# Skip term of a fused recurrent layer: a bf16 diagonal matmul and ScalarE seeds replaced by one fp32 VectorE pass per bank

## The chip, the cores and the metric

The kernel runs on the 8 cores of one Trainium2 chip. Each core works on two of the 16 sequences by itself; no core waits for another. The metric is the device time in microseconds (us) of the slowest core, median of three runs. The engines of a core are TensorE (PE, its weight loads PEld), VectorE (DVE), ScalarE (ACT), GpSimd (POOL) and SyncE (SP), which here only issues DMAs.

## What is computed

For x of shape (16, 2048, 2048), with all weights given:

```
xn = layernorm(x)
# recurrent layer on xn
xn1 = layernorm(xn) * gamma + beta
u   = xn1 @ W_in + b_in                  # (.., 8)
h_t = sigmoid(decay_logit) * h_(t-1) + u_t
x1  = xn + h @ W_out + b_out + xn1 * D_skip
xn2 = layernorm(x1) * gamma + beta
s   = x1 + relu(xn2 @ W_down + b_down) @ W_up + b_up
# quantized layer on the same xn
y   = relu(fake_quant(xn) @ fake_quant(kernel) + fake_quant(bias))
g   = silu(fake_quant(y))
out = x + s * g
```

`fake_quant` rounds to 8 bits with one scale per row (per column for the kernel).

## The kernel before

A core has 32 tiles of 128 rows of x; tile c is rows of sequence c % 2. The program writes five instruction queues by hand (`P` for PE, `V` for DVE, `S` for ACT, `G` for POOL, `Y` for SP): each `put` appends to one engine's queue and names marks that it waits for. Nothing is moved by a scheduler, so an engine runs its queue strictly in the written order, and the order of the calls in the loop `for i in range(1, NCH + 1)` is the schedule. Before the loop stands a prologue that quantizes and transposes the 2048 x 2048 kernel and works on tiles 0 to 2.

The steps of one tile c, with the names that the rest of the text uses:

- `load_x` fetches the tile (128 x 2048, fp32, 1 MB) into one of four buffers `x0` to `x3`.
- `v_stats` and `v_mean` (DVE) give mean and variance, `g_norm` (POOL, nine one-column operations, L451 to L461) the factors of both norms. `s_center` (ACT, L474) writes x minus mean into `xc`, one of two buffers.
- `g_z` (POOL, L465) writes the twice normalized row as bf16, `turn_z` transposes it by DMA into `zT`. `v_amax` (DVE, L481 to L485: a maximum over 2048 and four one-column operations), `s_quant_x` (ACT) and `g_ixb` (POOL, L494) give the integers of the quantized row, which a second DMA transposes into `ixT`.
- The quantized product: four banks q of 512 columns, each 16 matmuls 128x512 (`p_half`, `p_part`, L519) on top of the bias that `s_bias` (ACT, L501) writes into PSUM bank `py0` or `py1`; `v_evac` (DVE, L527) scales the bank into `t1` and keeps a running maximum. `v_ymax` and `s_gate` (ACT: Relu to 8 bits, L541, then Silu over all 2048 columns, L542) give the gate `g`.
- The recurrent part: `p_low` (16 matmuls, L570), `v_low` (L585, L588), a transpose `p_uT`, `v_scan` (DVE, L598: the same scan twice, once into fp32 `h`, once into bf16 `haug`), then the sum x1 in the four PSUM banks `px`: `s_seed` (ACT, L550 and L554) writes a starting value into each bank, `v_skip` (DVE, L562) multiplies banks 0 and 1 by `xc`, `p_skip` (PE, L578: 8 matmuls 128x128 of `zT` with a diagonal bf16 matrix) adds the skip term of banks 2 and 3, and `p_out` (PE, L605, L608) adds h @ W_out.
- The second norm: `s_square` (ACT, L615) sums the squares of `px`; `g_rstd2` (POOL, L624 to L628) makes the factor r2 of it; `v_hidden` (DVE, L632), a transpose `p_hfT` (PE, L637), `v_hfa` (DVE, L640) and `p_up` (PE, L646) add the last product to `px`.
- The end: `v_gated` (DVE, L653) multiplies `px` by the gate into `g`, bank by bank, `g_add` (POOL, L658) adds that to x, and `store` writes the tile.

There is one `px`, so tile c+1 can be seeded only when tile c has been gated. In a loop body i, the gate and the adds belong to tile i-1, the product to tile i, the quantization to tile i+1, the norms to tile i+2.

## Time and profile before

| | |
|---|---|
| median of 3 runs | 605.12 us (605.01 to 605.27) |
| the profiled execution | 605.74 us |
| span of its slowest core (7), first to last instruction | 604.2 us |
| spans of the other cores | 600.9 to 603.8 us |
| PE busy / share of the span | 553.4 us, 92% |
| DVE | 510.8 us, 85% |
| ACT | 518.8 us, 86% |
| POOL | 443.8 us, 73% |
| granted TensorE clock, mean of core 7 | 0.971; 1.00 from 100 to 580 us |

A row of a timeline is: start in us, duration in us, engine, line, operation, output <- input, shape, count; a bracket at the end tells how long the engine was idle before and what ended that. Instructions in a row of one kind are merged. The start of the next row minus the start of this one is what an instruction costs in its queue. The stages: the prologue until about 100 us, 30 tiles in a fixed rhythm until about 590 us, and the last tile's end.

### The profile page before, as it was taken

Reading aid. Unit: us, or ns where it says so; the run is one execution under the profiler, and the core shown is the slowest. Engines: PE = TensorE matmul, PEld = TensorE weight load, DVE = VectorE, ACT = ScalarE, POOL = GpSimd, SP = SyncE. Lnnn points to the kernel's source line nnn. Section 1 sums busy time; section 2 is a strip of 40 time slices with the busy share of each in tenths; the row PEclk is TensorE's granted clock in tenths of the full one; section 3 lists DMA queues with packets and bytes.
Section 4 is the critical chain, followed back from the end, with each engine's and each line's share of the span. In section 5 each row is a group of like instructions: output and inputs, shape, how many; then the busy total and the mean of one; then the engine's idle time right before and its main releaser. Section 6 shows DMA issues by size and latency. Waiting matters only on the chain.

```text
span 604.2 us, 10061 instructions; the slowest of 8 cores (600.9 to 604.2 us)
## 1 busy us (share of the span) xinstructions
PE 553.4 (92%) x3538; PEld 272.1 (45%) x3538; DVE 510.8 (85%) x1181; ACT 518.8 (86%) x497; POOL 443.8 (73%) x709
## 2 busy tenths in 40 slices
...
GB/s 240 335 347 312 220 132 68 190 201 205 209 196 198 200 190 178 195 205 209 182 183 194 199 194 200 209 197 206 195 178 202 182 201 209 191 191 183 132 71 140
DMA packets 141683, 118.89 MB, mean 197 GB/s; under 512 B 130368, under 2 KB 130368, under 8 KB 131520
## 3 DMA queue, kind: packets, MB, share of 16 engines
...
q8 instruction: 28, 0.46, 0.3%
q14 instruction: 23, 0.19, 0.1%
...
## 4 chain that ended last, share of the span: by engine, by line
PE 84%; ACT 6%; DVE 5%; DMA 2%; issue 1%; POOL 1%; SPq 0%; ACTq 0%; DVEq 0%; POOLq 0%
PE py L519 71%; PE pu L570 3%; PE px L646 3%; DMA x<-L_attn_x 2%; PE px L578 2%; DVE kst L333 1%; PE px L367 1%; PE px L608 1%; ACT xc L474 1%; DVE t L441 1%; PE pt L637 1%; ACT junk L350 1%; ACT zix L490 1%; ACT kq L389 1%; ACT k L350 1%
## 5 line engine op out<-in xcount | busy, mean ns | idle before, releaser
L519 PE MATMUL py<-kq,ixT 128*128 128x512 bf16 x2048 | 462.9, 380 | 3.6 <-ACT py L501 3.2
L519 PEld LDWEIGHTS py<-kq,ixT 128*128 128x128 bf16 x2048 | 194.3, 98 | 228.2 <-ACT py L501 12.9
L658 POOL TENSOR_TENSOR x<-x,g 128x512 f32<-128x512 f32 x124 | 155.1, 1272 | 56.6 <-DVE g L653 54.2
L615 ACT ACTIVATE junk<-px 128x2048 bf16<-128x2048 f32 x32 | 60.1, 1877 | 49.5 <-PE px L608 49.5
L527 DVE CUSTOM_DVE_ANT_0 t<-py,sc_bc,st 128x512 f32<-128x512 f32 x96 | 71.5, 745 | 21.7 <-PE py L519 21.6
L501 ACT ACTIVATE py<-brow,st 128x512 f32<-128x512 f32 x128 | 86.6, 677 | 3.8 <-DVE st L527 2.9
L441 DVE BATCH_NORM_STATS2 t<-x 128x6 f32<-128x512 f32 x128 | 81.5, 681 | 2.8 <-DMA x<-L_attn_x 2.8
L653 DVE TENSOR_TENSOR g<-px,g 128x512 f32<-128x512 f32 x124 | 77.0, 683 | 0.5 <-ACT g L542 0.5
L481 DVE TENSOR_REDUCE st<-xc 128x1 f32<-128x2048 f32 x32 | 72.8, 2275 | 2.2 <-ACT xc L474 2.2
L465 POOL TENSOR_SCALAR zix<-xc,ln 128x2048 bf16<-128x2048 f32 x32 | 65.4, 2045 | 3.7
L474 ACT ACTIVATE xc<-x,st 128x2048 f32<-128x2048 f32 x32 | 63.7, 1992 | 3.4 <-DVE st L447 3.4
L490 ACT ACTIVATE zix<-xc,c,st 128x2048 f16<-128x2048 f32 x32 | 66.5, 2078 | 0.0
L542 ACT ACTIVATE g<-q,st 128x2048 f32<-128x2048 uint8 x31 | 62.1, 2004 | 1.0
L541 ACT ACTIVATE q<-t,st 128x2048 uint8<-128x2048 f32 x31 | 61.7, 1990 | 0.0
L494 POOL TENSOR_SCALAR zix<-zix 128x2048 bf16<-128x2048 f16 x31 | 58.8, 1897 | 3.2 <-ACT zix L490 0.6
L562 DVE SCALAR_TENSOR_TENSOR px<-px,ln,xc 128x512 f32<-128x512 f32 x64 | 44.6, 742 | 0.0
L550 ACT ACTIVATE px<-spare,ln 128x512 f32<-128x512 f32 x64 | 41.1, 672 | 0.0
L554 ACT ACTIVATE px<-xc,ln 128x512 f32<-128x512 f32 x64 | 41.1, 671 | 0.0
L367 PE MATMUL px<-eye,junk 128*128 128x128 f16 x128 | 11.8, 265 | 24.6 <-POOL eyeb L229 16.2
L527 DVE CUSTOM_DVE_ANT_0 t<-py,sc_bc 128x512 f32<-128x512 f32 x32 | 22.1, 691 | 10.2 <-PE py L519 10.2
L632 DVE TENSOR_SCALAR hfS<-b,st 128x64 f32<-128x64 f32 x32 | 8.1, 254 | 25.8 <-POOL st L628 25.8
L570 PEld LDWEIGHTS pu<-wcat,zT 128*128 128x128 bf16 x512 | 18.9, 98 | 13.2 <-issue 12.7
...
## 6 DMA issues: line engine op xcount, KB each, us to landing
...
t<-L_ffn_kernelT SPq DMA_DIRECT2D x2, 1024.0 KB, 15.8
...
```

Source lines behind the costliest of these rows:

```text
L441: V.put(lambda e, q=q: e.bn_stats(t24[:, 6 * q:6 * q + 6], x_t[c % 4][:, 512 * q:512 * (q + 1)]), f"x{c}")
L465: G.put(lambda e: e.tensor_scalar(z_t, xc_t[c % 2][:], ln[:, 1:2], ln[:, 5:6], OP.mult, OP.mult), f"xc{c}", f"T_z{c - 1}_1" if c == 1 else ...
L474: S.put(lambda e: e.activation(xc_t[c % 2][:], x_t[c % 4][:], AF.Identity, bias=st[:, 2:3], scale=1.0), f"nm{c}", f"x{c}", f"z{c - 2}" if ...
L481: V.put(lambda e: e.tensor_reduce(st[:, 3:4], xc_t[c % 2][:], AX, OP.max, apply_absolute_value=True), f"xc{c}")
L490: S.put(lambda e: e.activation(ix16, xc_t[c % 2][:], AF.Identity, bias=c1536[:], scale=st[:, 4:5]), f"inv{c}", f"T_i{c - 1}_1" if c == 1 e ...
L501: S.put(lambda e: e.activation(py[q % 2][:], brow[:, 512 * q:512 * (q + 1)], AF.Identity, bias=0.0, scale=st[:, 5:6]), f"inv0_{c}", f"brow ...
L519: P.put(lambda e, j=j: e.matmul(bank[:], ixT[c % 2][:, 128 * j:128 * (j + 1)], kq[:, D * j + 512 * q:D * j + 512 * (q + 1)], start=False, ...
L527: V.put(lambda e: e.tensor_tensor_reduce(t1[:, 512 * q:512 * (q + 1)], py[q % 2][:], sc_bc[:, 512 * q:512 * (q + 1)], 1.0, 0.0 if q == 0 e ...
L541: S.put(lambda e: e.activation(q8[:], t1[:], AF.Relu, bias=0.0, scale=st[:, 13:14]), f"ym{c}", mark=f"q8_{c}")
L542: S.put(lambda e: e.activation(g_t[:], q8[:], AF.Silu, bias=0.0, scale=st[:, 14:15]), f"add{c - 1}" if c >= 1 else "kq16_15", prev=True, m ...
L653: V.put(lambda e, q=q: e.tensor_tensor(g_t[:, 512 * q:512 * (q + 1)], px[:, 512 * q:512 * (q + 1)], g_t[:, 512 * q:512 * (q + 1)], OP.mult ...
L658: G.put(lambda e: e.tensor_tensor(x_t[c % 4][:, 512 * q:512 * (q + 1)], x_t[c % 4][:, 512 * q:512 * (q + 1)], g_t[:, 512 * q:512 * (q + 1) ...
```

## The change

The skip term no longer goes through PE and ACT. ACT's `s_center` now writes the twice normalized x (fp32, buffer `zf`) in one pass, with scale and bias of the new `g_scale` (POOL). `v_skip` writes (gd + factor) * zf into a bank of `px` in one DVE pass; gd is a row of gamma * D_skip copied to all partitions, made for all four banks in the prologue, and lies with `zf` in SBUF. It is done for all four banks. `s_seed`, `p_skip` and the diagonal matrix are gone, with their POOL pieces in the prologue. `g_z` is a plain cast of `zf`. `g_norm` is divided in `g_scale` (three operations) and `g_norm` (six). The one-column operations of `v_amax` go to POOL as `g_scales` (five). The scan is done once on DVE, and `g_cast` (POOL) copies it to bf16. The Silu is two instructions of 1024 columns. x has a fifth buffer, `pre`, in which the prologue's small tensors lie at first; the statistics are taken one tile further ahead (tile i+3 in body i), with four sets of statistics, and `load_x(i + 4)` is issued right behind `store(i - 1)` and waits for it. The order of the loop is written anew.

```diff
-            G.put(lambda e: e.tensor_scalar(z_t, xc_t[c % 2][:], ln[:, 1:2], ln[:, 5:6], OP.mult, OP.mult),
+            G.put(lambda e: e.tensor_copy(z_t, zf_t[c % 2][:]),
...
-            S.put(lambda e: e.activation(xc_t[c % 2][:], x_t[c % 4][:], AF.Identity, bias=st[:, 2:3], scale=1.0),
...
+            S.put(lambda e: e.activation(zf_t[c % 2][:], x_t[c % 5][:], AF.Identity, bias=ln[:, 9:10], scale=ln[:, 8:9]),
...
+        def g_scales(c):
             st, ln = cell(c)
...
+            G.put(lambda e: e.tensor_scalar(st[:, 3:4], st[:, 3:4], TINY, None, OP.max), f"am{c}")
+            G.put(lambda e: e.tensor_scalar(st[:, 3:4], st[:, 3:4], 1.0 / 127.0, None, OP.mult), prev=True)
+            G.put(lambda e: e.tensor_tensor(st[:, 4:5], st[:, 3:4], cm1[:], OP.pow), prev=True, mark=f"inv{c}")
...
+        def v_skip(c, q):
+
             _, ln = cell(c)
...
+            V.put(lambda e: e.scalar_tensor_tensor(px[:, 512 * q:512 * (q + 1)], gdr[:, 512 * q:512 * (q + 1)], ln[:, 6:7],
+                                                   zf_t[c % 2][:, 512 * q:512 * (q + 1)], OP.add, OP.mult),
+                  f"xc{c}", f"ln{c}", f"gdr{q}", f"px_init{q}" if c == 0 else f"sg{c - 1}_{q}", mark=f"sk{c}_{q}")
...
+            v_hidden(i - 1)
+            if m:
+                v_units(i)
                 p_half(i, 0, 1)
...
+            p_hfT(i - 1)
+            if m:
+                p_part(i, 1, 0, 6)
...
+            v_hfa(i - 1)
+            p_up(i - 1)
...
+            v_gated(i - 1, 0)
+            v_skip(i, 0)
+            v_gated(i - 1, 1)
+            v_skip(i, 1)
+            g_add(i - 1, 0)
...
```

The order of POOL's queue moves. One loop body from the first add of a tile (L658) over the quantization (L494) to the factor r2 (L628), with the next norm behind it, before:

```order
L658 TENSOR_TENSOR x0<-x0,g 128x512 [waits s_dve]
L494 TENSOR_SCALAR zix<-zix 128x2048 [waits s_act]
L658 TENSOR_TENSOR x0<-x0,g 128x512 [waits s_dve] x3
L624 TENSOR_SCALAR st0<-b33 128x1 [waits s_dve]
L626 TENSOR_SCALAR st0<-st0 128x1 [waits s_pool]
L627 TENSOR_TENSOR st0<-st0 128x1 [waits s_act,s_pool]
L628 TENSOR_TENSOR st0<-st0,cneg 128x1 [waits s_pool]
L451 TENSOR_SCALAR ln2<-st2 128x1 [waits s_dve]
L454 TENSOR_TENSOR ln2<-ln2,cneg 128x1 [waits s_pool]
L455 TENSOR_TENSOR ln2<-st2,ln2 128x1 [waits s_pool]
```

The same stretch of the changed kernel, first part: the first add (L640), `g_scale` (L444 to L447), the quantization (L493), `g_cast` (L581), the second add, and `g_norm` (L452 on):

```order
L640 TENSOR_TENSOR x0<-x0,g 128x512 [waits s_dve]
L444 TENSOR_SCALAR ln2<-st2 128x1
L446 TENSOR_TENSOR ln2<-ln2,cneg 128x1 [waits s_pool]
L447 TENSOR_SCALAR ln2<-st2,ln2 128x1 [waits s_pool]
L493 TENSOR_SCALAR zix<-zix 128x2048 [waits s_act]
L581 CAST haug0<-h0 128x128 [waits s_dve,s_pe]
L640 TENSOR_TENSOR x0<-x0,g 128x512
L452 TENSOR_SCALAR ln2<-st2 128x1
L453 TENSOR_TENSOR ln2<-ln2,cneg 128x1 [waits s_pool]
L454 TENSOR_TENSOR ln2<-ln2 128x1 [waits s_pool]
L455 TENSOR_TENSOR ln2<-ln2 128x1 [waits s_pool]
L456 TENSOR_TENSOR ln2<-ln2 128x1 [waits s_pool]
```

The last part of that stretch, one body earlier: the end of `g_norm`, the adds of banks 2 and 3, `g_z` (L460), r2 (L611), then `g_scales` (L480 to L485):

```order
L457 TENSOR_TENSOR ln1<-ln1 128x1 [waits s_pool]
L640 TENSOR_TENSOR pre<-pre,g 128x512 [waits s_dve] x2
L606 TENSOR_SCALAR st3<-b33 128x1 [waits s_dve]
L608 TENSOR_SCALAR st3<-st3 128x1 [waits s_pool]
L460 CAST zix<-zf1 128x2048 [waits s_act,d_z0,s_pool]
L610 TENSOR_TENSOR st3<-st3 128x1 [waits s_act,s_pool]
L611 TENSOR_TENSOR st3<-st3,cneg 128x1 [waits s_pool]
L480 TENSOR_SCALAR st1<-st1 128x1 [waits s_dve]
L481 TENSOR_SCALAR st1<-st1 128x1 [waits s_pool]
L482 TENSOR_TENSOR st1<-st1,cm1 128x1 [waits s_pool]
L483 TENSOR_SCALAR st1<-st1,ln1 128x1
L485 TENSOR_TENSOR st1<-st1,ln1 128x1 [waits s_pool]
```

Before, nothing but the quantization stood between a tile's first add and r2 besides the adds themselves, and norm and `g_z` came behind r2; now `g_scale`, `g_cast`, `g_norm` and `g_z` stand ahead of r2.

DVE's queue at the gate (L653) of a tile and the skip passes (L562) of the next, before:

```order
L653 TENSOR_TENSOR g<-px,g 128x512 [waits s_act]
L653 TENSOR_TENSOR g<-px,g 128x512 x3
L527 ISA t1,st2<-py1,sc_bc,st2 128x512 [waits s_pe,s_dve]
L527 ISA st2 128x1
L598 SCALAR_TENSOR_TENSOR haug1<-decay,h3,pt 128x128
L598 SCALAR_TENSOR_TENSOR h1<-decay,h3,pt 128x128
L562 SCALAR_TENSOR_TENSOR px<-px,ln2,xc1 128x512 [waits s_act] x2
L441 BN_STATS t24<-x3 128x6 [waits d_x3]
L441 BN_STATS t24<-x3 128x6
```

The same place of the changed kernel, from `v_hidden` (L615) on; `spare` holds the row gd, `zf0` the normalized x:

```order
L615 TENSOR_SCALAR hfS<-b33,st1 128x2x32 [waits s_pool]
L564 TENSOR_TENSOR uS<-pu,c40 128x4x8 [waits s_pe]
L567 TENSOR_SCALAR a33<-pu,ln2 128x32
L526 ISA t1,st2<-py0,sc_bc 128x512 [waits s_pe,s_act]
L526 ISA st2 128x1
L623 TENSOR_SCALAR hfaug<-pt,ccol 128x128 [waits s_pe]
L635 TENSOR_TENSOR g<-px,g 128x512 [waits s_pe,s_act]
L550 SCALAR_TENSOR_TENSOR px<-spare,ln2,zf0 128x512 [waits s_dve]
L635 TENSOR_TENSOR g<-px,g 128x512
L550 SCALAR_TENSOR_TENSOR px<-spare,ln2,zf0 128x512 [waits s_dve]
L576 SCALAR_TENSOR_TENSOR h2<-decay,h0,pt 128x128 [waits s_pe]
L526 ISA t1,st2<-py1,sc_bc,st2 128x512 [waits s_pe]
```

Gate (L635) and skip pass (L550) now alternate; the scan and one evacuation stand between banks 1 and 2, and banks 2 and 3 follow in the same way. Both tensor inputs of a skip pass are in SBUF, where one was in PSUM.

## Rows read from the trace of the kernel before

**Rows 1.** One tile's period: stretch, length, busy us of PE, PEld, DVE, ACT, POOL.
```profile
316.13:332.27 16.14, 16.14 (x100) 7.56 (x99) 14.20 (x36) 14.60 (x15) 12.73 (x20) 1.00 0.73 196
```
**Rows 2.** Timeline of PE over one period: start, duration, line, operation.
```profile
318.53 0.30 PE L637 MATMUL pt<-cst,hfS 128*128 128x128 f32 x1
318.67 1.89 PE L519 MATMUL py<-kq,ixT 128*128 128x512 bf16 x8
320.49 0.60 PE L646 MATMUL px<-wup,hfaug 33*128 33x512 bf16 x4
321.02 0.71 PE L570 MATMUL pu<-wcat,zT 128*128 128x73 bf16 x16
...
330.32 0.61 PE L578 MATMUL px<-spare,zT 128*128 128x128 bf16 x8
330.86 0.18 PE L605 MATMUL pu<-wg,haug 9*128 9x33 bf16 x1
...
331.20 3.63 PE L519 MATMUL py<-kq,ixT 128*128 128x512 bf16 x16
334.67 0.29 PE L637 MATMUL pt<-cst,hfS 128*128 128x128 f32 x1
```
**Rows 3.** Timeline of POOL over one period.
```profile
318.44 0.57 POOL L454 TENSOR_TENSOR ln<-ln,cneg 128x1 f32<-128x1 f32 x1
...
321.43 2.04 POOL L465 TENSOR_SCALAR zix<-xc,ln 128x2048 bf16<-128x2048 f32 x1
325.01 1.28 POOL L658 TENSOR_TENSOR x<-x,g 128x512 f32<-128x512 f32 x1 [1.53 <-DVE g L653]
326.38 1.90 POOL L494 TENSOR_SCALAR zix<-zix 128x2048 bf16<-128x2048 f16 x1
328.35 3.72 POOL L658 TENSOR_TENSOR x<-x,g 128x512 f32<-128x512 f32 x3
332.17 0.26 POOL L624 TENSOR_SCALAR st<-b 128x1 f32<-128x1 f32 x1
...
333.45 0.19 POOL L627 TENSOR_TENSOR st<-st 128x1 f32<-128x1 f32 x1 [0.70 <-ACT junk L615]
333.72 0.57 POOL L628 TENSOR_TENSOR st<-st,cneg 128x1 f32<-128x1 f32 x1
```
**Rows 4.** Timeline of DVE over one period.
```profile
319.90 0.34 DVE L640 TENSOR_SCALAR hfaug<-pt,ccol 128x128 bf16<-128x128 f32 x1
...
324.23 2.48 DVE L653 TENSOR_TENSOR g<-px,g 128x512 f32<-128x512 f32 x4
327.18 0.75 DVE L527 CUSTOM_DVE_ANT_0 t<-py,sc_bc,st 128x512 f32<-128x512 f32 x1 [0.46 <-PE py L519]
...
328.24 0.46 DVE L598 TENSOR_TENSOR_SCAN h<-decay,h,pt 128x128 f32<-128x128 f32 x1
328.62 1.39 DVE L562 SCALAR_TENSOR_TENSOR px<-px,ln,xc 128x512 f32<-128x512 f32 x2
...
334.32 0.25 DVE L632 TENSOR_SCALAR hfS<-b,st 128x64 f32<-128x64 f32 x1 [0.70 <-POOL st L628]
```
**Rows 5.** Timelines of DVE and POOL at two places of the prologue, not in order.
```profile
34.61 1.29 DVE L290 TENSOR_SCALAR decay<-decay,dec 128x128 f32<-128x128 f32 x1
33.84 1.97 POOL L347 TENSOR_SCALAR junk<-xc,kst 128x2048 f16<-128x2048 f32 x1
51.24 0.90 DVE L394 TENSOR_TENSOR bq<-bcf,kst 128x4 f32<-128x4 f32 x1
50.85 1.27 POOL L249 TENSOR_TENSOR cst<-cst,gsum 128x512 f32<-128x512 f32 x1
L394 DVE TENSOR_TENSOR bq<-bcf,kst x4: 141/153/898, 45.6 to 75.4; 128x4 f32<-128x4 f32 x4
```
**Rows 6.** Timelines of POOL and ACT where tile 1 begins.
```profile
75.38 1.04 POOL L264 CAST wup<-zT 128x1024 bf16<-128x1024 f32 x1
74.84 2.00 ACT L474 ACTIVATE xc<-x,st 128x2048 f32<-128x2048 f32 x1
```

More of the change, by code:

```diff
@@ L24 @@
 NU = 73
-NB = 2
 class Queue:
@@ L461, in g_norm @@
[L461 removed]
+            G.put(lambda e: e.tensor_scalar(ln[:, 1:2], st[:, 1:2], EPS, None, OP.add))
+            G.put(lambda e: e.tensor_tensor(ln[:, 2:3], ln[:, 1:2], cneg[:], OP.pow), prev=True)
+            G.put(lambda e: e.tensor_tensor(ln[:, 3:4], ln[:, 0:1], ln[:, 8:9], OP.mult), prev=True)
+            G.put(lambda e: e.tensor_tensor(ln[:, 4:5], ln[:, 1:2], ln[:, 2:3], OP.mult), prev=True)
@@ L694, in build_nc @@
             load_k(n)
-        for c in range(1, 4):
+        for c in range(1, 5):
             load_x(c)
@@ L723, in build_nc @@
         v_mean(0)
+        g_scale(0)
         g_norm(0)
@@ L733, in build_nc @@
         v_amax(0)
+        g_scales(0)
         step(2)
@@ L785, in build_nc @@
         v_mean(1)
+        g_scale(1)
         g_norm(1)
@@ L826, in build_nc @@
         v_mean(2)
-        g_norm(2)
-        s_center(2)
-        s_bias(1, 1)
+        g_scale(2)
+        v_units(0)
+        p_uT(0)
+        v_evac(0, 2)
+        s_bias(1, 0)
+        v_skip(0, 0)
+        v_skip(0, 1)
+        v_scan(0)
+        g_cast(0)
+        v_skip(0, 2)
+        v_skip(0, 3)
+        p_half(0, 3, 1)
+        p_out(0)
+        s_center(2)
+        v_proj(0)
+        g_norm(2)
+        g_rstd2(0, 0)
+        s_square(0)
+        v_stats(3, 0)
+        v_stats(3, 1)
@@ L876, in build_nc @@
+            d, b, a, m = i + 3 < NCH, i + 2 < NCH, i + 1 < NCH, i < NCH
+            v_evac(i - 1, 3)
+            v_ymax(i - 1)
+            if m:
+                s_bias(i, 1)
+                s_gate(i - 1)
+                p_half(i, 0, 0)
+                p_low(i)
+            if a:
+                v_amax(i + 1)
+                g_scales(i + 1)
+            v_hidden(i - 1)
+            if m:
+                v_units(i)
                 p_half(i, 0, 1)
-                v_low(i)
+            p_hfT(i - 1)
@@ L900, in build_nc @@
-            if b:
-                v_stats(i + 2, 0)
-            if m:
-                v_proj(i)
-                g_rstd2(i)
-            if b:
-                v_stats(i + 2, 1)
-            if m:
-                v_evac(i, 2)
+            v_hfa(i - 1)
+            p_up(i - 1)
+            if not m:
+                last(i - 1)
+                continue
+            s_bias(i, 2)
+            if a:
+                s_quant_x(i + 1)
+            p_part(i, 1, 6, 8)
+            p_uT(i)
+            p_half(i, 1, 1)
@@ new lines, in build_nc @@
+            v_gated(i - 1, 0)
[3 more added lines that the diff above has]
+            g_add(i - 1, 0)
+            if b:
+                g_scale(i + 2)
+            if a:
+                g_ixb(i + 1)
+            v_scan(i)
+            g_cast(i)
+            v_evac(i, 1)
+            s_bias(i, 3)
+            v_gated(i - 1, 2)
+            v_skip(i, 2)
+            v_gated(i - 1, 3)
+            v_skip(i, 3)
+            g_add(i - 1, 1)
+            if b:
+                g_norm(i + 2)
+                s_center(i + 2)
@@ L909, in build_nc @@
+            g_add(i - 1, 2)
+            g_add(i - 1, 3)
+            store(i - 1)
+            if i + 4 < NCH:
+                load_x(i + 4)
+            p_half(i, 2, 0)
+            p_half(i, 2, 1)
+            p_part(i, 3, 0, 4)
+            p_out(i)
+            p_part(i, 3, 4, 16)
+            v_evac(i, 2)
             if a:
                 s_bias(i + 1, 0)
-            if b:
-                v_mean(i + 2)
-                s_center(i + 2)
-                g_norm(i + 2)
-            if a:
-                s_bias(i + 1, 1)
```

293 lines of the change are left out of this document (97 added, 196 removed).

## Prediction

> **What bounds the kernel now.** I read first one period of the rhythm, engine by engine [rows 1]: PE is busy for all of its 16.14 us, ACT 14.60, DVE 14.20, POOL 12.73. The period shows in any line: the transpose L637 stands at 318.53 and 334.67 [rows 2]. So PE sets the pace, and a part that leaves PE is worth its whole cost, if the others keep up. Then I read each engine's timeline for what it waits for. POOL waits twice per tile: 1.53 us for the gate of the tile (DVE L653) and 0.70 us for the sum of squares [rows 3]; the rest of its period is filled. DVE waits 0.70 us for r2 from POOL and some tenths for PE [rows 4]. What is not in the busy sums is order: r2 stands on POOL about 9.3 us behind the first add of the tile before (325.01 to 334.29) and in front of the norm and `g_z` [rows 3].
>
> **What leaves PE.** `p_skip` starts at 330.32 and the next matmul at 330.86: 0.54 us per tile. With some 0.05 us of waiting for `hfaug` a period of PE alone would be 15.6 us.
>
> **What goes to the others.** ACT loses four seeds and has room: no term. DVE gains two skip passes (1.39 for two, [rows 4]) and loses one scan (0.46) and five one-column operations: its load stays near 14.5 to 15. POOL gains `g_scales` (five operations) and `g_cast`. A one-column operation costs its duration and a gap of 0.08: L627 starts at 333.45, lasts 0.19, and L628 starts at 333.72 [rows 3]. So 0.27 to 0.34, and 0.65 for a pow (0.57 long). `g_scales` is 4 x 0.3 + 0.65 = 1.8, the small cast at most 0.3. POOL's work rises from 13.9 (16.14 - 1.53 - 0.70) to about 15.7 us. Alone that would just fit.
>
> **The term that decides: a closed chain.** In the new order r2 stands last. Take the gate of tile i-1 (bank 0) as zero:
> - to the first add: 0.78 (324.23 in [rows 4], 325.01 in [rows 3]).
> - POOL, in written order, to the end of r2. Four adds, three of which take 3.72, with 0.10 before the next: 5.1. The quantization, 326.38 to 328.35: 1.97. `g_z` is now a cast; a cast of half the size lasts 1.04 [rows 6], and L465, which it replaces, 2.04 [rows 3]: 1.95. `g_cast`: 0.25. Thirteen one-column operations (three in `g_scale`, six in `g_norm`, four for r2), three of them pows: 3 x 0.65 + 10 x 0.30 = 4.9. Sum 14.1.
> - r2's end (334.29) to `v_hidden` 0.03, to the transpose L637 0.35 (334.32 [rows 4], 334.67 [rows 2]), 0.14 until the matmul behind it may start (318.53, 318.67), then the six matmuls that now stand between it and `p_up`: 16 of them took 3.47 (331.20 to 334.67), so 1.30. `p_up` lasts 0.60 and DVE starts some 0.05 later. Sum 2.5. DVE reaches `v_hfa` in the same time (one evacuation, 0.75, stands ahead of it), and `v_hfa` to `p_up` is 0.59 (319.90, 320.49).
>
> That is the next gate: 0.8 + 14.1 + 2.5 = **17.4 us**, more than 16.14. Each link is in the written order or a named wait, so nothing overlaps it away; before, the same chain was 0.8 + 9.3 + 2.5, less than a period, and the ring was opened by the ready gate. `g_scales` is not in it: it runs in the 3.3 us outside. Without pipelining gaps the stretch on POOL is 13.5, which makes 16.8.
>
> **The second term: both inputs of a skip pass in SBUF.** [Rows 5] show DVE operations beside POOL operations. L394, a tensor_tensor of 4 columns with both inputs in SBUF, lasts 0.15 us, but 0.90 once: it starts at 51.24 while POOL is in L249, and ends at 52.14, POOL at 52.12. L290, 128 columns from SBUF to SBUF, lasts 1.29: it starts at 34.61 in POOL's L347 and ends at 35.90, POOL at 35.81. So such an operation does not run beside a POOL operation; it waits for its end. In the rhythm of before there is none: L653 and L562 read one of their inputs from PSUM. Now there are four a tile, 512 columns each, right where POOL has its adds and the quantization. No row shows the other direction, POOL waiting for DVE. Its price lies between nothing and four passes of 0.74, 3.0 us a tile. I take it that what excludes one excludes the other, and follow the order: the first skip starts at 0.72 (its gate of 0.68 done), just before the add at 0.78, which is then 0.6 late; the second, ready at 2.1, waits for that add until about 2.65 and holds POOL back 0.55; the third waits for the quantization until about 6.35 and costs POOL 0.45; the fourth waits for the second add, 0.5. A pass that has waited needs some 0.6 more of its 0.74, as L394 and L290 end at once. Sum 2.1: the chain is **19.45 us**.
>
> The Trainium skill says the same of both directions (SBUF — State Buffer, "Who interferes with whom"): a VectorE instruction with two SBUF inputs and a GpSimd instruction that reads SBUF take one shared port pair, the one that starts first for its whole length, and the other fully blocks. [Rows 5] agree for VectorE, 0.90 against 0.15 us; by the page alone the sum would be the one above, by the rows alone anything from 17.4 to 20.4.
>
> The same exclusion lengthens a second ring. Gates and skips of four banks: each gate 0.68 + 0.04, each skip 0.65 to the next, 5.5; scan and evacuation between them 1.1; so `p_out` can start 6.7 after the gate. On PE from there to `p_up`: 0.34, 34 matmuls of 0.217, `p_low` 0.56, transpose 0.14: 8.4, and 0.7 to the gate. That is 15.8 without exclusion, and with the four waits (2.4 on DVE) 18.2. So the order of POOL alone is not all that stands against the change.
>
> **The ends.** Tile 1's centring (ACT, at 74.84) waits now for `g_scale`, which POOL reaches after L264 at 76.4 and ends 1.3 later: ACT's queue, with the last pieces of the kernel behind it, is up to 2.9 late [rows 6]. The statistics of tile 3 (four passes) and two more skips stand ahead of tile 0's last evacuation, the x4 load ahead of tile 1's transposes. I take 5 us, between 2 and 8. At the end body 30 has neither norm nor `g_z` and follows the second ring, 2 us more than now; the last tile about 1 us more. `load_x` waits for its store on SP with the transpose of z behind it: 4 to 5 us late, but z is needed a whole body later, no cost.
>
> **The sum**, against the profiled execution (605.74, its span 604.2 and 1.5 around it; the median of the runs is 605.12): 29 gaps of 19.45 - 16.14 = 3.31 are 96, and 5 + 2 + 1: 104. 605.1 + 104 = **709 us**.
>
> **Rivals.**
> - *POOL's chain without the exclusion's second side.* DVE waits for POOL, but POOL is not held back. For it: no row shows POOL waiting. 17.4 us: 29 x 1.2 + 5 = 40, so 645; with 16.8 it is 629, and half of the delay gives 680.
> - *PE stays the bound, the change is a gain.* It needs POOL's stretch from first add to r2 within 12.3 us (15.6 - 0.8 - 2.5) instead of 14.1, and skip passes that do not collide: if casts and one-column operations on POOL cost less in this order than the rows say, the 0.54 us per tile come through: 605 - 30 x 0.54 + 5 = 594. Where it ends between, 12.3 to 12.8, the prologue eats it and the time is 600 to 606.
> - *DVE starves.* POOL's instructions follow each other with hardly a gap (adds start 1.24 apart and last 1.27). If a waiting pass gets its turn only when POOL waits, the third and fourth pass come behind later adds, and the last skip near 13 instead of 9; the sum of squares, behind the centring on ACT, then ends near 18 and the chain is 21.5: 605 + 29 x 5.4 + 8 = 770.
> - *A slight loss*, 606 to 622, if the chain closes at 16.2 to 16.6.
>
> **Numbers.** Forecast (682 to 745) 0.52, the first rival (622 to 682) 0.24, PE or near it (590 to 606) 0.11, starving above 745 0.06, slight loss 0.07. The range 622 to 745 leaves out the last three but some at their edges. A measurement of this kernel tells apart about 0.2% (1.2 us): faster 0.07, same 0.04, slower 0.89.
>
> **What would show it.** The period between two gates, 19.5; 17.4 and unchanged POOL durations for the first rival; 15.6 to 16.1 for the second. POOL should wait only for the gate (about 1.6 us less) and DVE for r2, PE some 3 us for `hfS`. If exclusion is real, L550 shows well over 0.74 us in its mean, and adds or casts over 1.27 and 1.9. Adds at 1.27 with L550 long would say that only DVE waits. PE's granted clock should stay at the 1.00 (2.4 GHz) of [rows 1]. The prediction is wrong if r2 is ready before L637 is reached.

## The result, and the profile after

The changed kernel takes 706.93 us (median of 4 runs, 705.74 to 707.29), the kernel before beside it 605.19: a ratio of 1.1675, with a 95% interval of 1.1657 to 1.1694. Slower by 17%, as forecast (709, range 622 to 745). The profiled execution has a span of 705.8 us on core 1; the other cores have 697.6 to 705.4 and show the same two periods. In some executions the cores of a die run at a lower clock; every ratio in this document leaves such executions out.

The line of busy times of the profile's page, and two periods from gate to gate (stretch, length, busy us of PE, PEld, DVE, ACT, POOL, granted clock, DMA share, GB/s; they answer to [rows 1]):

```profile
PE 592.5 (84%) x3290; PEld 267.2 (38%) x3290; DVE 582.6 (83%) x1053; ACT 455.4 (65%) x402; POOL 537.6 (76%) x899
```
```profile
315.76:335.20 19.44, 17.97 (x92) 7.59 (x91) 16.59 (x31) 12.94 (x13) 15.72 (x25) 0.91 0.62 168
335.20:354.20 19.00, 16.50 (x92) 7.07 (x91) 16.43 (x31) 12.99 (x12) 15.79 (x25) 1.00 0.71 159
```

No engine is busy for its whole period any more. There are two kinds of period, 19.00 and 19.44, in no fixed order; the 29 gaps between the gates at 104.13 and 661.72 have a mean of 19.23, against 16.14 before. That is 90 of the 102 us. The first gate comes 6.0 later than before (104.13 against 98.10), the last gap (661.72 to 683.24) is 5.0 longer than its like before, the last tile 1.1. The start and the last gap differ from core to core: on six of the other cores the last gap is 18.35 to 18.36, so much of the 5.0 belongs to the slowest core alone.

**The period of 19.00.** POOL from the gate's first add (L640) to r2 (L611), rows that answer to [rows 3]:

```profile
335.97 1.27 POOL L640 TENSOR_TENSOR x<-x,g 128x512 f32<-128x512 f32 x1 [1.94 <-DVE g L635]
337.33 0.52 POOL L444 TENSOR_SCALAR ln<-st 128x1 f32<-128x1 f32 x1
...
338.58 0.73 POOL L447 TENSOR_SCALAR ln<-st,ln 128x1 f32<-128x1 f32 x1
...
341.35 0.62 POOL L581 CAST haug<-h 128x128 bf16<-128x128 f32 x1
...
348.78 1.89 POOL L460 CAST zix<-zf 128x2048 bf16<-128x2048 f32 x1
350.75 0.19 POOL L610 TENSOR_TENSOR st<-st 128x1 f32<-128x1 f32 x1
351.02 0.57 POOL L611 TENSOR_TENSOR st<-st,cneg 128x1 f32<-128x1 f32 x1
```

DVE in the same tile; the wait in brackets is the end of the chain:

```profile
335.20 0.69 DVE L635 TENSOR_TENSOR g<-px,g 128x512 f32<-128x512 f32 x1 [0.95 <-ACT py L500]
335.93 1.87 DVE L550 SCALAR_TENSOR_TENSOR px<-spare,ln,zf 128x512 f32<-128x512 f32 x1
...
351.62 0.25 DVE L615 TENSOR_SCALAR hfS<-b,st 128x64 f32<-128x64 f32 x1 [1.12 <-POOL st L611]
...
354.20 0.69 DVE L635 TENSOR_TENSOR g<-px,g 128x512 f32<-128x512 f32 x1 [1.20 <-PE px L629]
```

Gate to add 0.77, add to the end of r2 15.62 (335.97 to 351.59), from there to the next gate 2.61: the closed chain of the prediction, link by link. The forecast was 0.8, 14.1 plus 2.1 of exclusion, and 2.5.

**The period of 19.44.** PE in the tile before (start, duration), and the granted clock in four stretches of it:

```profile
322.60 0.40 PE L589 MATMUL px<-wout,haug 9*128 9x512 bf16 x3
324.38 0.38 PE L589 MATMUL px<-wout,haug 9*128 9x512 bf16 x1 [1.38 <-DVE px L550]
324.70 6.18 PE L518 MATMUL py<-kq,ixT 128*128 128x512 bf16 x20
330.72 0.70 PE L557 MATMUL pu<-wcat,zT 128*128 128x73 bf16 x16
...
344.14 4.49 PE L518 MATMUL py<-kq,ixT 128*128 128x512 bf16 x20
```
```profile
322.60:324.70 2.10, 0.72 (x6) 0.19 (x6) 2.06 (x3) 0.34 (x1) 1.93 (x3) 1.00 0.83 155
324.70:327.30 2.60, 2.60 (x10) 1.06 (x10) 2.60 (x7) 2.60 (x3) 2.29 (x6) 0.73 0.41 76
327.30:330.70 3.40, 3.40 (x12) 1.35 (x11) 2.17 (x8) 2.63 (x4) 3.15 (x5) 0.70 0.39 164
330.70:335.20 4.50, 4.50 (x37) 2.18 (x36) 3.03 (x7) 4.47 (x5) 2.70 (x8) 1.00 0.58 177
```

PE waits 1.38 us for the last skip pass. Then its clock is at the lower of its two levels, 1.2 GHz, for part of 20 matmuls (means of 0.73 and 0.70), and these take 6.02 us (324.70 to 330.72) instead of 4.33 in the next tile. In such a tile r2 is ready at 332.14 and v_hidden starts at 332.27 without a wait, behind a v_amax that PE's late bank has held back; PE's ring sets the period. At full clock it would be 19.44 - 1.69 = 17.75 (an estimate from these rows).

**The exclusion** is in the page's groups:

```profile
L550 DVE SCALAR_TENSOR_TENSOR px<-spare,ln,zf 128x512 f32<-128x512 f32 x128 | 155.4, 1215 | 4.4
L447 POOL TENSOR_SCALAR ln<-st,ln 128x1 f32<-128x1 f32 x32 | 22.5, 702 | 3.3
```

The skip passes last 1.215 us in the mean, where 0.74 was the duration of an undisturbed one, and POOL's L447 lasts 0.70 where a one-column operation of its kind took 0.26. That suggests that each side waits for the other; the first two experiments test it. ACT now has room: it is busy for 12.9 of 19.0 us.

### The profile page after: what moved, and what is told of

Read it like the earlier page. It is cut to its first block, busy times and chain, and to the rows that moved or that the text cites. A ratio compares the mean times of both kernels' runs of the same rounds, so it can differ in the third digit from the quotient of the medians.

```text
span 705.8 us, 9594 instructions; the slowest of 8 cores (697.6 to 705.8 us)
## 1 busy us (share of the span) xinstructions
PE 592.5 (84%) x3290; PEld 267.2 (38%) x3290; DVE 582.6 (83%) x1053; ACT 455.4 (65%) x402; POOL 537.6 (76%) x899
## 4 chain that ended last, share of the span: by engine, by line
PE 33%; DVE 28%; POOL 26%; issue 7%; DMA 3%; ACT 2%; SPq 0%; DVEq 0%; POOLq 0%; ACTq 0%
PE py L518 26%; DVE px L550 12%; POOL x L640 8%; DVE g L635 7%; POOL zix L460 4%; PE px L629 3%; POOL pre L640 2%; DMA x<-L_attn_x 2%; DVE kst L325 2%; DVE t L526 2%; POOL ln L447 2%; PE pu L557 1%; POOL haug L581 1%; POOL ln L446 1%; POOL st L611 1%
## 5 line engine op out<-in xcount | busy, mean ns | idle before, releaser
L518 PE MATMUL py<-kq,ixT 128*128 128x512 bf16 x2048 | 504.2, 398 | 7.6 <-DMA ixT<-zix 3.6
L640 POOL TENSOR_TENSOR x<-x,g 128x512 f32<-128x512 f32 x100 | 126.4, 1275 | 52.6 <-DVE g L635 52.6
L550 DVE SCALAR_TENSOR_TENSOR px<-spare,ln,zf 128x512 f32<-128x512 f32 x128 | 155.4, 1215 | 4.4
L635 DVE TENSOR_TENSOR g<-px,g 128x512 f32<-128x512 f32 x124 | 84.7, 683 | 32.9 <-PE px L629 30.1
L469 ACT ACTIVATE zf<-x,ln 128x2048 f32<-128x2048 f32 x26 | 54.4, 2094 | 73.8 <-DVE px L550 68.0
L475 DVE TENSOR_REDUCE st<-zf 128x1 f32<-128x2048 f32 x32 | 72.8, 2277 | 4.5 <-ACT zf L469 4.5
L544 ACT ACTIVATE g<-q,st 128x1024 f32<-128x1024 uint8 x62 | 67.8, 1140 | 1.0
L489 ACT ACTIVATE zix<-zf,c,st 128x2048 f16<-128x2048 f32 x32 | 66.5, 2080 | 0.2 <-POOL st L482 0.2
L460 POOL CAST zix<-zf 128x2048 bf16<-128x2048 f32 x32 | 60.5, 1889 | 2.2
L589 PE MATMUL px<-wout,haug 9*128 9x512 bf16 x128 | 25.4, 383 | 42.5 <-DVE px L550 42.4
L493 POOL TENSOR_SCALAR zix<-zix 128x2048 bf16<-128x2048 f16 x31 | 59.1, 1907 | 2.5
L640 POOL TENSOR_TENSOR pre<-pre,g 128x512 f32<-128x512 f32 x24 | 31.0, 1304 | 10.1 <-DVE g L635 10.1
L359 PE MATMUL px<-eye,junk 128*128 128x128 f16 x128 | 11.8, 265 | 24.3 <-POOL eyeb L226 15.8
L447 POOL TENSOR_SCALAR ln<-st,ln 128x1 f32<-128x1 f32 x32 | 22.5, 702 | 3.3
## 6 DMA issues: line engine op xcount, KB each, us to landing
zf<-L_ffn_kernelT SPq DMA_DIRECT2D x2, 1024.0 KB, 16.9
```

The lines of the kernel that those rows point to most:

```text
L460: G.put(lambda e: e.tensor_copy(z_t, zf_t[c % 2][:]), f"xc{c}", f"T_z{c - 1}_1" if c == 1 else f"zT{c - 1}" if c else None, prev=True, mar ...
L475: V.put(lambda e: e.tensor_reduce(st[:, 3:4], zf_t[c % 2][:], AX, OP.max, apply_absolute_value=True), f"xc{c}", f"pb{c - 4}_3" if c >= 4 e ...
L489: S.put(lambda e: e.activation(ix16, zf_t[c % 2][:], AF.Identity, bias=c1536[:], scale=st[:, 4:5]), f"inv{c}", f"T_i{c - 1}_1" if c == 1 e ...
L518: P.put(lambda e, j=j: e.matmul(bank[:], ixT[c % 2][:, 128 * j:128 * (j + 1)], kq[:, D * j + 512 * q:D * j + 512 * (q + 1)], start=False, ...
L544: S.put(lambda e, f=f: e.activation(g_t[:, f], q8[:, f], AF.Silu, bias=0.0, scale=st[:, 14:15]), (f"add{c - 1}" if h else f"add{c - 1}_1") ...
L550: V.put(lambda e: e.scalar_tensor_tensor(px[:, 512 * q:512 * (q + 1)], gdr[:, 512 * q:512 * (q + 1)], ln[:, 6:7], zf_t[c % 2][:, 512 * q:5 ...
```

## Experiments

A ring is a chain of steps from one tile's gate to the next tile's gate, each of which waits for the one before. The exclusion is the prediction's second term: a VectorE pass with both inputs in SBUF and a GpSimd operation do not run at the same time. The theory on trial: three rings lie close together (POOL's, 19.0; PE's, 17.75 or with the lower clock 19.44; DVE's from the gate to the end of v_amax and on to p_up, 17.8), and the exclusion lengthens each of them. Rivals: the order alone, the exclusion alone, or PE and its clock alone. Every ratio below is to the kernel before, run beside it on the same chip, and the times are medians of four executions if no other number is given.

### The exclusion taken away, and put into the kernel before

```
-  e.scalar_tensor_tensor(px[..], gdr[..], ln[:, 6:7], zf_t[..], OP.add, OP.mult)
+  e.scalar_tensor_tensor(px[..], px[..], ln[:, 6:7], zf_t[..], OP.is_le, OP.mult)
```

> The changed kernel, in which the skip pass (L550) reads px, which lies in PSUM, where it read the row gd in SBUF; its shape, its place and its waits stay. The starting value with gd is left out, so the skip term is not the reference's. No pass has both inputs in SBUF any longer, so the exclusion between VectorE and GpSimd falls away, while the order of both queues stays. Theory (the order of POOL's queue and the exclusion together): in the changed kernel's trace the ring on POOL takes 19.0 us from gate to gate (335.20 to 354.20), of which I put 1.4 to 1.6 on the exclusion (one-column operations of 0.51 and 0.73 where they last 0.19 and 0.26 alone, a cast of 0.62 that should be 0.29). So a period of 17.4 to 17.6, as the prediction had it for the order alone; the ring over gates, skips, scan, p_out and the 34 matmuls falls from 19.4 (half clock in it) to about 15.9 and PE keeps a clock of 1.00; 29 gaps x 1.7 less: 650 to 660 us. Skip passes near 0.74 us in the mean. Rival 1 (the exclusion is real but costs nothing, since the order of POOL decides): 700 to 707. Rival 2 (the exclusion is all that costs, the order nothing): 600 to 622.

e1: 653.33 us, ratio 1.0785 (1.0766 to 1.0803). All 29 gaps are 17.55 to 17.58. Its trace, groups of the page (busy us, mean ns of one), and POOL's rows:

```profile
L550 DVE SCALAR_TENSOR_TENSOR px<-px,ln,zf 128x512 f32<-128x512 f32 x128 | 96.9, 759 | 4.4
```
```profile
280.59 1.27 POOL L640 TENSOR_TENSOR x<-x,g 128x512 f32<-128x512 f32 x1 [1.66 <-DVE g L635]
281.94 0.19 POOL L444 TENSOR_SCALAR ln<-st 128x1 f32<-128x1 f32 x1
...
282.87 0.26 POOL L447 TENSOR_SCALAR ln<-st,ln 128x1 f32<-128x1 f32 x1
...
294.19 0.57 POOL L611 TENSOR_TENSOR st<-st,cneg 128x1 f32<-128x1 f32 x1
```

With one input in PSUM the same instruction lasts 0.76, and POOL's short operations are back at 0.19 and 0.26. From the first add to the end of r2 it is 14.17 (280.59 to 294.76); the prediction's sum for it was 14.1. So the exclusion costs 1.44 of a period on POOL's ring, and the order alone gives 17.56. PE's granted clock is 1.00 in all these periods. Of the 102 us, 54 go with the exclusion (the lower clock of the changed kernel among them) and 48 stay with the order. The rival that had no cost for it, and the one that had all the cost in it, both fall.

```
 # the kernel before, v_skip of banks 0 and 1
-  e.scalar_tensor_tensor(px[..], px[..], ln[:, 8:9], xc..)
+  e.scalar_tensor_tensor(px[..], gdr[..], ln[:, 8:9], xc..)
```

> The kernel before, in which the two skip passes of banks 0 and 1 (L562) read the row in SBUF from which the seeds are made, not the seed in PSUM; the seeds still run, the order and the number of operations stay. The factor that the seed adds is left out in these two banks. So two passes a tile get two SBUF inputs and nothing else changes. Theory (exclusion in both directions): these passes start beside the third and fourth add on POOL (328.35 to 332.07, adds back to back) and wait for an add's end, about 1 to 1.3 us each, so p_out of these banks and of those behind is later by 1.5 to 2.5 us; the factor r2 of the tile before is late by up to two passes. PE has 15.6 of 16.14 filled, so most of that shows: 620 to 650 us. L562 over 1.1 us in the mean (0.69 before). Rival (only DVE waits, and the order has room for it): 605 to 612 with L562 long. Rival (no exclusion for such passes; the time of the changed kernel comes from the order alone): 604 to 607 with L562 at 0.7.

e7: 626.48 us, ratio 1.0343 (1.0323 to 1.0363); the period goes from 16.14 to 16.82. Nothing but the place of one input changed, in two passes a tile. Groups of its page:

```profile
L658 POOL TENSOR_TENSOR x<-x,g 128x512 f32<-128x512 f32 x124 | 184.4, 1507 | 65.7 <-DVE g L653 63.4
L562 DVE SCALAR_TENSOR_TENSOR px<-spare,ln,xc 128x512 f32<-128x512 f32 x64 | 77.4, 1255 | 0.0
```

The adds, which lasted 1.26 to 1.28 without exception before ([rows 3] have the like), now have a mean of 1.51 and a maximum of 1.81, and the passes 1.26. This is the direction for which the kernel before had no row: POOL waits for DVE. The rival "only DVE waits" falls.

### The orders

```
 # e3_out_late
-            p_part(i, 3, 0, 4)
+            p_part(i, 3, 0, 12)
             p_out(i)
-            p_part(i, 3, 4, 16)
+            p_part(i, 3, 12, 16)
```

> The changed kernel, in which p_out stands eight matmuls later in PE's queue (behind twelve of the last bank's sixteen, not behind four); nothing else moves. PE no longer waits 1.4 us there for the skip passes, and the ring gate, skips, p_out, remaining matmuls, p_up shortens by eight matmuls, 1.7 us, to about 16. Theory of three rings: the ring on POOL stays at 19.0 and sets every period; PE's granted clock stays at 1.00 in the steady part because its wait ahead of p_out is gone; the periods of 19.43 fall to 19.0: 29 x 0.22 = 6 and a part of the last gap, together 695 to 702 us. Rival (PE's ring with its half clock is what bounds the kernel, POOL only follows): 640 to 680. If the clock falls with the waits of PE in general, not with this one, the drop moves to another place and the time stays at 700 to 707.

e3: 696.39 us, ratio 1.1498 (1.1478 to 1.1518). The gaps are 19.00 but for one of 20.07, and the last is 16.83 instead of 21.52; the granted clock is 1.00 in the periods of 19.00. So PE's ring and its lower clock cost 10.5 us of the 102 (in the gaps of the two profiles 10.1: 15 periods longer by 0.43, and 4.7 in the last gap; the one of 20.07 gives 1.1 back), and behind them POOL's 19.00 stands as it was. The clock is not the cause of most of the loss.

```
 # e2_r2_first
                 v_mean(i + 3)
+            g_rstd2(i, 1)
             if b:
                 g_z(i + 2)
                 turn_z(i + 2)
-            g_rstd2(i, 1)
```

> The changed kernel, in which the last two operations of the factor r2 stand ahead of g_z on POOL where they stood behind it; nothing else moves. The ring on POOL loses the cast of 2048 columns, 1.9 us plus its gap: from 19.0 to 17.0. Theory of three rings: what is late next is DVE's own ring, 15.3 us from gate to the end of the maximum plus 2.6 to the next gate, 17.8, and PE's ring, 17.8 at full clock and 19.4 as it stands with the 20 matmuls behind p_out at half clock. So 17.8 to 19.4 a period, 665 to 700 us: less than the 29 x 2.0 = 58 us that POOL's ring gives. Rival (POOL's ring alone sets the pace): 17.0 to 17.3 a period, 645 to 658 us. Rival (the place of r2 doesn't matter because PE's ring or the exclusion sets it): 704 to 708.

e2: 704.11 us, ratio 1.1608 (1.1567 to 1.1648): a miss. The cast of 1.9 us left POOL's ring, and the time hardly moved. Periods of 19.43 remain where PE has the lower clock, and the others came only to 18.77, not 17.8. Why, DVE and POOL show:

```profile
290.60 2.28 DVE L475 TENSOR_REDUCE st<-zf 128x1 f32<-128x2048 f32 x1
292.79 1.22 DVE L615 TENSOR_SCALAR hfS<-b,st 128x64 f32<-128x64 f32 x1
```
```profile
291.44 0.57 POOL L611 TENSOR_TENSOR st<-st,cneg 128x1 f32<-128x1 f32 x1
292.08 1.89 POOL L460 CAST zix<-zf 128x2048 bf16<-128x2048 f32 x1
```

v_hidden (L615) lasts 1.22 instead of 0.25: it starts inside g_z's cast and ends with it (294.01 and 293.97). The move had made a new collision. It has one tensor input only, in SBUF, and writes SBUF. That it is this, and not something else in the 18.77, the next two kernels test.

> The changed kernel with both moves of order at once: the last two operations of r2 ahead of g_z on POOL, and p_out eight matmuls later on PE; the exclusion stays. Theory (three rings and a second collision): in the kernel with r2 first the ring on DVE measured 18.77 us in its tiles at full clock; 1.0 of it was v_hidden (L615, both operands in SBUF), which lasted 1.22 us instead of 0.25 since it came to lie beside the cast of g_z on POOL. Its other tiles took 19.43 through PE at half clock, and p_out later takes these away. So every period 18.8 and the last gap 17: 104.2 + 29 x 18.78 + 17 + 22 and 2 around the span, 686 to 692 us, with L615 at 1.1 to 1.3 in the mean. Rival 1 (POOL's ring of 17.0 is what is left, the collision of L615 costs nothing): 640 to 655. Rival 2 (DVE's ring without the collision, 17.8): 658 to 665.

e4, both edits above at once: 689.96 us, ratio 1.1384 (1.1366 to 1.1402), gaps of 18.75 to 18.77 but for one of 19.75, L615 at 1.145 in the mean. As expected.

```
 # e9_z_last, besides both edits
                 g_scales(i + 1)
+                if i >= 2:
+                    g_z(i + 1)
+                    turn_z(i + 1)
...
-            if b:
-                g_z(i + 2)
-                turn_z(i + 2)
```

> As the kernel with both moves of order, and g_z with its transpose stands one place further back: behind g_scales, so that it ends about where the next tile's gate begins. v_hidden then no longer lies beside the cast. Theory: L615 falls from 1.2 to 0.25 us and DVE's ring from 18.8 to 17.8; against it the cast now ends 0.3 to 0.4 us behind the point at which the next first add and the first skip pass would start, which may give back up to 0.6. So a period of 17.8 to 18.5: 658 to 682 us. Rival (the 18.8 come from elsewhere, from POOL's load or PE): 686 to 692, unchanged.

e9: 682.38 us, ratio 1.1261 (1.1242 to 1.1279), 0.4 above the upper edge of what was expected. L615 is back at 0.246 in the mean. The periods are now 17.79 to 17.80 where nothing is late, which is DVE's ring as put down beforehand, 18.1 where the cast runs into the next add, and 19.3 to 19.6 where PE's clock falls:

```profile
308.80:328.32 19.52, 17.88 (x92) 7.73 (x91) 16.84 (x31) 13.80 (x14) 16.80 (x26) 0.91 0.61 180
328.32:346.12 17.80, 16.34 (x92) 6.96 (x91) 16.41 (x32) 11.40 (x11) 14.58 (x25) 1.00 0.66 161
```

So the collision of L615 was worth 18.77 - 17.80 = 0.97, and with it gone the lower clock is back and makes 11 of the periods 19.3 to 19.6.

The Trainium skill has the rule for this collision too (SBUF — State Buffer, "Who interferes with whom"): a VectorE tensor_scalar can run in a mode that takes both port pairs and then shuts GpSimd out, or is shut out. The rows agree that L615 and the cast do not run together: 1.22 beside it, 0.25 away from it. In which mode L615 ran no row shows.

### Everything taken away at once

Input from px, both moves of order, g_z behind g_scales:

> All causes that the theory names taken away at once: skip passes that read px in PSUM instead of the row gd (the starting value is left out, so the skip term is not the reference's), r2 ahead of g_z, g_z behind g_scales, p_out eight matmuls later. Theory: the ring on POOL is 0.8 + 12.3 + 2.5 = 15.6 us, the one on DVE 13.4 + 2.6 = 16.0, the one on PE 15.9 to 16.0. So periods of 16.0 to 16.2, as long as those of the kernel before although PE has 0.54 us less work: 104.2 + 30 x 16.1 + 21.4 + 2, 606 to 614 us. If anything that the theory does not name makes the changed kernel slow (the fifth buffer, the load behind its store, more operations on POOL), it stays here: over 625.

e10: 623.19 us, ratio 1.0278 (1.0258 to 1.0298), 9 us more than expected but under the 625 named for an unknown cause. The shortest periods are 16.00 to 16.05, as worked out. Others are longer by a wait that the sums had left out; PE's rows of a tile of 19.25:

```profile
244.31 1.04 PE L518 MATMUL py<-kq,ixT 128*128 128x512 bf16 x4
247.09 3.44 PE L518 MATMUL py<-kq,ixT 128*128 128x512 bf16 x8 [1.75 <-ACT junk L596]
...
264.80 1.89 PE L518 MATMUL py<-kq,ixT 128*128 128x512 bf16 x8 [0.21 <-DMA ixT<-zix]
```

These eight are the next tile's first matmuls and need ixT, which a DMA transposes behind g_ixb. In a period of 19 us it is mostly ready in time; in the two tiles after this one it is 0.21 and 0.43 late, in later ones up to 1.40. Behind the wait of 1.75 the clock falls. The profile names the sum of squares as its end, which these matmuls don't need; SP's rows of the same stretch show what was late:

```profile
236.81 0.34 SPq L428 DMA_DIRECT2D x<-L_attn_x  x1
237.24 5.34 SPq L464 DMA_TRANSPOSE zT<-zix  x1
242.68 1.77 SPq L494 DMA_TRANSPOSE ixT<-zix  x1
```

The integers were ready at 241.29, but the transpose of z, issued 0.4 us behind the 1 MB load, held the queue until 242.6. A transpose of ixT lands 4.3 us after its issue in this stretch, here at about 247.0, and the matmuls start at 247.09. In five more tiles ixT was issued 0.7 to 2.2 us behind its integers in the same way, and PE waited 1.05 to 2.57; in most others it was issued 0.1 behind them and PE waited 0.2 to 0.5. So in the longest tiles PE waits for SP's queue, where the load stands ahead of the transposes. No run moved that load alone.

### The start

The load of tile 4 behind the transposes of tile 1 on SP's queue, all else as changed:

> The changed kernel, in which only the load of tile 4 in the prologue stands behind the two transposes of tile 1 on SP's queue instead of ahead of them. Theory: of the 6.0 us by which the first gate is later than before (104.13 against 98.10), up to 3.4 are PE's wait for ixT at 96.28, since the transposes queue behind 1 MB; without it the first gate comes at 101 to 102 and the time is 2 to 3 us less, 703 to 705. Rival (the transposes are late because their source is): 706 to 707.5.

e15: 704.59 us, ratio 1.1628 (1.1603 to 1.1653), as expected; the first gate at 101.97 instead of 104.13. SP's rows in the changed kernel, then here:

```profile
85.11 0.33 SPq L428 DMA_DIRECT2D pre<-L_attn_x  x1
85.51 6.26 SPq L464 DMA_TRANSPOSE zT<-zix  x1
```
```profile
86.47 2.27 SPq L464 DMA_TRANSPOSE zT<-zix  x1
88.79 2.27 SPq L494 DMA_TRANSPOSE ixT<-zix  x1
91.17 1.00 SPq L428 DMA_DIRECT2D pre<-L_attn_x  x1
```

Behind 1 MB the transpose held the queue for 6.26 us, and for 2.27 ahead of it. That is 2.2 of the 6.0 us by which the start is late; no run takes the rest apart.

### The steps of the change in the old order

The runs so far say: keep r2 right behind the adds, keep an input of every pass in PSUM. ACT has the room to write the starting value. So the loop was written in the order of the kernel before, with the steps of the change. In short, not word for word:

```
+        s_seed(c): px[bank q] = Identity(gdr[bank q] + ln[:, 6:7]), four banks, ACT
-  v_skip: scalar_tensor_tensor(px, gdr, ln[:, 6:7], zf, add, mult)
+  v_skip: tensor_tensor(px, px, zf, mult)
   loop: v_evac 3, v_ymax, v_hfa, v_amax and its scales (DVE), v_units, v_evac 0,
         gates 0-3, v_evac 1, v_scan, skips 0-3, statistics of i+3, v_evac 2, v_hidden
   POOL: add 0, g_ixb, add 1, g_cast, adds 2-3, r2, g_scale(i+3), g_norm(i+3), g_z
```

> The whole computation of the changed kernel (no p_skip, no bf16 diagonal, zf in full precision, fifth buffer, one scan and its cast), in the order of the kernel before: r2 right behind the adds, g_scale and g_norm of tile i+3 and g_z behind it, v_hidden and its transpose at the end of a body, the gate four passes in a row, then the skips. ACT writes the starting value (gd + factor) into all four banks of px and the skip pass multiplies px by zf, so no pass has both inputs in SBUF; the one-column operations of v_amax are back on DVE. Theory: r2 is ready about 10 us behind the gate, the ring on POOL is 13 us and no longer sets the pace; ACT has 14.8 us of work, DVE 14.6, POOL about 14.3, PE 15.6 to 15.85: a period of 15.6 to 16.1, a start 3 to 6 us later than before: 592 to 609 us. If the causes named so far were not the causes, or the extra pieces on POOL alone were too much: over 620.

e13: 620.94 us, ratio 1.0248 (1.0227 to 1.0268): a miss, outside the 592 to 609 expected and 1 us over the 620 that was named as a sign against the causes found so far. POOL's ring is gone, but the period is 16.39, the first gate at 106.3. PE waits 0.5 a tile for a bias that stands behind the quantization on ACT. The next two runs keep this order and change only places in it.

> The kernel with the whole computation in the old order, with four edits that its trace asks for. (1) s_bias(i,2) stands on ACT ahead of s_quant_x(i+1): PE waited 0.5 us a tile for it, behind 2.1 us of quantization. (2) The load of tile 4 stands on SP behind the transposes of tile 1; there zT took 6.15 us behind the load's 1 MB and PE waited 2.1 us for ixT. (3) In the prologue s_square(0) stands ahead of s_center(2), r2 of tile 0 ahead of g_z(2), and the statistics of tile 3 in body 1. (4) g_scale(1) stands ahead of the wup piece, and gdrow(1) ahead of s_center(1). Theory: the period of 16.39 loses the 0.5 and comes to PE's own 15.85 to 15.95, where ACT's 15.0 fits; the first gate comes at 100 to 103 instead of 106.3. 101.5 + 30 x 15.9 + 21.5 + 2 = 602, range 597 to 609, so level with the kernel before or 1% faster. Rival (ACT is the bound and the 0.5 are ACT's own wait for p_out, 1.0 us): the period stays at 16.2 to 16.4, 611 to 618.

e14: 626.48 us, ratio 1.0339 (1.0323 to 1.0355): slower, a miss. The start improved as meant (first gate 101.80), but the period rose to 16.69. The 0.5 us of PE's wait had been no loss: it lay in front of a longer ring, gate, evacuation, scan, four skips, p_out, 16 matmuls, transpose, 8, p_up, p_low, 8, evacuation, gate. And the bias ahead of the quantization made g_ixb, and behind it r2, 0.3 later against the gate than in e13 (the expectation of the next run has 0.6). POOL's wait for the quantization and DVE's for r2 in one tile:

```profile
322.75 1.90 POOL L493 TENSOR_SCALAR zix<-zix 128x2048 bf16<-128x2048 f16 x1 [0.88 <-ACT zix L489]
```
```profile
330.33 0.25 DVE L630 TENSOR_SCALAR hfS<-b,st 128x64 f32<-128x64 f32 x1 [0.60 <-POOL st L626]
```

> The tuned kernel in the old order (whole computation, seeds by ACT), with three more moves. Its trace at 16.69 a period shows two things late in one ring (gate, evacuation, scan, four skips, p_out, 16 matmuls, transpose, 8 matmuls, p_up, p_low, 8 matmuls, evacuation, gate): PE waited 0.30 for the last skip and 0.30 for hfS, which waited for r2, and r2 was 0.6 later than in the version before since the quantization on ACT, and g_ixb behind it, had become later (POOL waited 0.88 for it). So now (1) the second add stands ahead of g_ixb and fills that wait, r2 0.9 earlier; (2) the scan stands ahead of the evacuation of bank 1, which waited 0.47 for PE, so that the skips start 0.35 earlier; (3) the evacuation of bank 2 stands ahead of the second half of the statistics, so that ACT's bias for the next tile doesn't wait 0.66. Theory: PE waits for nothing, a period of 15.9 to 16.15, first gate at 101.8: 101.8 + 30 x 16.0 + 21.5 + 2 = 605, range 600 to 611. That is level with the kernel before: its ring had two skips and the 0.54 of p_skip, this one four skips. Rival (the ring is not what bounds the old order, ACT's or PE's load is): 620 to 627, unchanged.

e17: **603.80 us (7 runs), ratio 0.9963 (0.9949 to 0.9976)**: within the range expected, and 0.4% under the kernel before, so in practice level with it. The three moves were not run one by one. 19 of its 30 gaps are 15.74 to 15.77, the mean is 15.98 (16.16 before). The longest are 16.4 to 16.9, most of them with a wait of PE for ixT, as this one (246.29 to 263.23):

```profile
257.67 1.89 PE L518 MATMUL py<-kq,ixT 128*128 128x512 bf16 x8 [1.02 <-DMA ixT<-zix]
```

So the shortest period nearly reached what the prediction had as PE's share alone, 15.6. Of 0.38 a tile (11 us) that this would bring, the later start (101.93 against 98.10) takes 3.8 and the longer gaps some 6.

Last (e16), the kernel of e14 with the changed kernel's own skip pass, gd row and zf both in SBUF, and no seeds:

> The tuned kernel in the old order, but with the skip pass of the changed kernel: gd row and zf both in SBUF, no seeds on ACT. So the whole computation, ACT with 2.5 us less work a tile, and the exclusion of four passes a tile against POOL in an order in which r2 stands right behind the adds. Theory: of the four passes, which come about 4 us behind the gate, beside quantization, adds and cast, each waits 0.4 to 1.2 us and each is waited for by POOL: for two passes in the kernel before it was 0.68 us a period and 1.1 us on DVE, so for four 1.2 to 2 us: DVE 14.8 + 1.9 = 16.7 us of work, a period of 16.7 to 17.6: 625 to 655 us. Rival (with r2 early the exclusion has room, and less work on ACT helps): 597 to 612.

745.67 us, ratio 1.2308 (1.2288 to 1.2327): a miss by 90 us, slower than the changed kernel. DVE's passes in e14, then rows of DVE and POOL here:

```profile
323.83 2.47 DVE L565 TENSOR_TENSOR px<-px,zf 128x512 f32<-128x512 f32 x4
```

```profile
333.19 5.37 DVE L565 SCALAR_TENSOR_TENSOR px<-spare,ln,zf 128x512 f32<-128x512 f32 x4
```
```profile
334.06 1.58 POOL L655 TENSOR_TENSOR x<-x,g 128x512 f32<-128x512 f32 x1
335.59 0.75 POOL L596 CAST haug<-h 128x128 bf16<-128x128 f32 x1
336.30 3.38 POOL L655 TENSOR_TENSOR x<-x,g 128x512 f32<-128x512 f32 x2
```
```profile
338.93:344.04 5.11, 5.11 (x18) 2.01 (x18) 3.28 (x9) 4.28 (x4) 3.62 (x10) 0.67 0.50 205
```

Four passes back to back take 5.3 us where they take 2.4 with px as input, all of it in the ring named above, and PE's waits (1.06 us for the cast that they hold back, 1.28 for the last of them) are followed by 16 matmuls at a mean clock of 0.67, 5.1 us instead of 3.5. 2.9 + 1.6 - 0.6 of waits that went = 3.9, and the period is 20.5 after 16.7. The step that failed: the expectation costed the exclusion by DVE's load, not by the ring through it, and had no term for the clock.

## Why the prediction was right, and where it was not

- **The closed chain through r2** (17.4): right. With the exclusion taken away it measured 17.56. It set the pace in 14 of the 29 periods only: in the 15 others, those of 19.44, r2 is ready before PE reaches the transpose, which the prediction named as its sign of being wrong. Without the lower clock (e3) it set all but one.
- **The exclusion, both directions** (+2.1): right in kind, 0.7 too large: 1.44. The step that failed is who goes first. The prediction had the first skip go before the add, "which is then 0.6 late". In the trace the skip at 335.93 waits (1.87) for the add at 335.97, which lasts its usual 1.27. POOL's lost time is instead in its short operations, against their durations in e1: L444 0.33, L447 0.47, the cast L581 0.33, L452 0.32, which is 1.45. The sign that the prediction gave would have misled: the adds stay at 1.27 with L550 long, which it read as "only DVE waits". The small operations, not the adds, have to be looked at.
- **The second ring** on PE (15.8, with exclusion 18.2): 17.75 at full clock. The words "PE's granted clock should stay at the 1.00" were wrong; the lower clock makes it 19.44, and it, not POOL, bounds half of the tiles. That the sum still came out, 19.45 for 19.23, is luck in part: 0.7 too much exclusion, 0.16 too little chain, and a missing term for the clock (0.23). Of the signs named for PE, a wait of some 3 us for `hfS` was wrong too: it is 1.03, and 1.38 for the last skip.
- **The ends** (5 + 2 + 1): 6.0, 5.0 and 1.1. Of the 5.0 of the last gap 2.9 are again the clock: 20 matmuls take 7.27 us (671.48 to 678.75) instead of 4.33; moving p_out, which takes PE's wait and the lower clock away together, gave 4.7 back. For the start the steps named are seen in the trace: ACT's centring of tile 1 waits 2.86 for g_scale, what that costs no run shows; the load ahead of the transposes is worth 2.2 (e15).
- **What hides the rest**: "no cost" for the later load_x held in periods of 19 us; in those of 16 PE waits for ixT in some tiles, because the load stands ahead of the transposes on SP (e10). DVE's own ring at 17.8 was not in the prediction; with the collision of L615 it is why r2's place alone gave only 3 us (e2).
- **The rivals**: the first one's numbers (17.4, 645) are those of e1, which has no exclusion in either direction; that DVE alone waits, e7 refutes. "PE stays the bound" was wrong for this order, and the reason given, 14.1 against the 12.3 that it needs, is what the old order repaired. "DVE starves" did not happen here, nor in e16, whose period of 20.5 has another cause: its four passes get their turn within 5.4 us, and PE's lower clock comes on top.

The Trainium skill's rule that the exclusion works in both directions (SBUF — State Buffer, "Who interferes with whom") is borne out by e7's adds at up to 1.81 instead of 1.27. The same section says that the one that issues first has the ports and the other waits; the recorded starts do not show that order, since the skip pass starts 0.04 us before the add and is the one that waits.
